# A two-FFN transformer block on one core: the low halves of the second FFN's gate and up products by seven products in place of eight

## The reference

```python
x = x + 0.5 * ffn(layernorm(x), w_gate_up, w_proj)
x = x + attention(layernorm(x), w_qkv, w_proj, b_proj)      # linear attention, 16 heads of 32
x = x + 0.5 * ffn(layernorm(x), w_gate_up, w_proj)

def ffn(x, w_gate_up, w_proj):
    wq = ternary_quant(w_gate_up)            # groups of 64: +-scale or 0, in bf16
    gate, up = split(x @ wq.T)               # 512 -> 2 x 2048
    h = silu(gate) * up
    hn = rms_norm(h)
    return hn @ ternary_quant(w_proj).T      # 2048 -> 512
```

## Time and profile before

| | us |
|---|---|
| median of 3 runs | 875.66 |
| lowest, highest run | 872.84, 879.67 |
| the profiled execution | 873.84 |
| its span, first to last instruction | 871.2 |
| PE busy | 852.2 |
| DVE busy | 511.7 |
| ACT busy | 443.0 |
| POOL busy | 71.5 |

### The profile page before, as it was taken

One profiled execution on the slowest core, in us unless ns is written; L12 is line 12 of the kernel. 1 busy time (PEld: TensorE's weight loads), 2 busy tenths in 40 slices (PEclk: granted clock), 3 DMA queues, 4 the chain that ended last, 5 costly groups with the idle time before them and its releaser, 6 DMA issues. The chain is left out here.

```text
span 871.2 us, 13142 instructions
## 1 busy us (share of the span) xinstructions
PE 852.2 (98%) x4932; PEld 413.3 (47%) x4998; DVE 511.7 (59%) x979; ACT 443.0 (51%) x822; POOL 71.5 (8%) x114
## 2 busy tenths in 40 slices
PE   6999999999999989999999999999999999999998
PEld 5544444444444434464646464444444444444445
DVE  7999997824347566657696958433443443432332
ACT  7976667536435555556657463543444344334331
POOL 2211001200010010000000000000000000000000
PEclk9999999999999999999999999999999999999999
DMA  9999508996747679960505062163433343333236
GB/s 262 179 182 125 76 1 169 216 223 185 163 117 149 112 147 196 185 125 1 86 1 86 1 147 97 21 113 73 73 73 72 73 73 73 73 73 61 61 69 136
DMA packets 257486, 94.70 MB, mean 109 GB/s; under 512 B 242832, under 2 KB 245648, under 8 KB 256400
## 3 DMA queue, kind: packets, MB, share of 16 engines
q1 hardware_dynamic: 248448, 73.42, 45.2%
q0 software_dynamic: 5024, 13.11, 6.7%
q10 hardware_dynamic: 3952, 7.34, 2.6%
HBM read 29.62 MB, written 8.39 MB: 44 GB/s over the span
## 5 line engine op out<-in xcount | busy, mean ns | idle before, releaser
L1643 PE MATMUL proj_ps<-down_w,slots 128*128 128x512 bf16 x910 | 202.9, 379 | 1.1 <-issue 0.2
L1172 DVE SCALAR_TENSOR_TENSOR slots<-up_ps,silu 128x512 f32<-128x512 f32 x117 | 80.9, 691 | 179.8 <-PE up_ps L1629 134.2
L1629 PE MATMUL gate_ps<-gu_w,xT 128*128 128x512 bf16 (+1 forms) x762 | 173.1, 368 | 3.1 <-ACT silu L809 2.3
L1629 PE MATMUL up_ps<-gu_w,xT 128*128 128x512 bf16 (+1 forms) x759 | 171.3, 366 | 0.9
L1643 PEld LDWEIGHTS proj_ps<-down_w,slots 128*128 128x128 f16 x928 | 90.7, 98 | 109.9 <-DVE xs L1194 0.8
L809 ACT ACTIVATE silu<-gate_ps 128x512 f32<-128x512 f32 x117 | 68.8, 588 | 142.9 <-PE gate_ps L1629 142.9
L819 ACT ACTIVATE o_buf<-slots 128x512 f32<-128x512 f32 x128 | 80.5, 629 | 113.7 <-DVE slots L1172 113.0
L1629 PEld LDWEIGHTS gate_ps<-gu_w,xT 128*128 128x128 f16 x776 | 74.0, 98 | 88.4 <-ACT silu L809 2.7
L1629 PEld LDWEIGHTS up_ps<-gu_w,xT 128*128 128x128 f16 x776 | 73.7, 98 | 84.4 <-issue 0.8
L1185 DVE SCALAR_TENSOR_TENSOR slots<-slots,inv 128x512 f16<-128x512 f32 x124 | 91.0, 744 | 3.7 <-ACT slots L830 3.6
L830 ACT ACTIVATE slots<-slots,inv 128x512 f16<-128x512 f32 x124 | 86.3, 711 | 11.1 <-POOL inv L709 7.6
(11 more groups left out here) (151 smaller groups left out, 942.4 us busy)
## 6 DMA issues: line engine op xcount, KB each, us to landing
gu_kept<-gu_w POOLq DMA_DIRECT2D x4, 1024.0 KB, 4.7
gu_w<-gu_kept POOLq DMA_DIRECT2D x4, 1024.0 KB, 6.2
out_dram<-xs SPq DMA_DIRECT2D x15, 256.0 KB, 2.4
xs<-in_L_attn_x_dram SPq DMA_DIRECT2D x3, 1024.0 KB, 8.5
aw<-in_L_attn_w_qkv_dram ACTq DMA_DIRECT2D x12, 256.0 KB, 2.9
slots<-in_L_ffn_w_gate_up_dram ACTq DMA_DIRECT2D x5, 512.0 KB, 6.7
aw<-in_L_ffn_w_gate_up_dram POOLq DMA_DIRECT2D x10, 256.0 KB, 5.5
aw<-in_L_ffn_w_proj_dram POOLq DMA_DIRECT2D x8, 256.0 KB, 5.5
```

The source lines that it names most:

```text
L1172: nc.vector.scalar_tensor_tensor(out=h_rows(i, q), in0=bank(up_ps, j), scalar=gu_out(i), in1=silu_rows(j), op0=ALU.mult, op1=ALU.mult).the ...
L1629: mm = nc.tensor.matmul(bank(ps, j)[:, first:first + width], xT(m)[:, t, r, k, :], gu_w[:, q, side, k, first:first + width], start=(k + r ...
L1643: mm = nc.tensor.matmul(proj_ps[:, use % 2, :], h_turned(i)[:, r, j, :], down_w[:, j, :], start=(r + j == 0), stop=(r == 1 and j == HC - 1))
```

## The change

The two low halves of x of two tiles, A = (a1 a2; b1 b2) with 256 rows of K each, times the gate and up weights (G1 U1; G2 U2) are a 2 x 2 product of blocks. The change makes it by seven products (Strassen's form in Winograd's order) in place of eight, for tiles 18 to 31 taken in pairs: 28 sets of one pair and one column block. A product is two matmuls of 512 columns; the high halves stay as they were, 16 matmuls a set. PE's step k makes the high products of set k (`x`, `y`, `v`, `w`, one PSUM bank each) between the low products of set k + 1.

The sums inside a set are made in PSUM: product 1 stands in bank y, ACT copies it to bank x (`seed_x`), products 6 and 5 are added in y with a copy kept after each (`hold_two` on DVE, `hold_four` on ACT), DVE writes the seed of bank w (`seed_w`) and adds to bank v (`join_v`).

It needs sums of the weights (four forms of 128x1024 per column block) and of x. The weight forms are made in tiles 8 to 10 of the first FFN (`weight_parts` on ACT, `weight_forms` on DVE), scaled by a power of two of the largest group mean (a second `partition_all_reduce` on POOL, behind `inverse(7)`), stored in DRAM (`keep_forms`, 4 x 1 MB) and brought back after attention (`bring_forms`). `low_halves(u)` makes the sums of x, five DVE operations for each pair. `row_sum`, `keep_weights` and all else of tiles 8 to 15 keep their places. `xT8` moves from `att_w` to a slot.

```diff
+SETS = 4 * (LAYER - 2) // 2
+FIRST_LOW = (1, 7, 6, 5, 2, 3, 4)
+IN_STEP = (1, 7, "x", 6, "y", 5, "v", 2, 3, "w", 4)
+LOW_BANK = {1: "y", 6: "y", 5: "y", 3: "y", 2: "x", 7: "v", 4: "v"}
...
@@ pool
+            pool.wait_ge(most_done, 1)
+            nc.gpsimd.partition_all_reduce(w_all, w_most, P, bass.bass_isa.ReduceOp.max).then_inc(all_done, 1)
             for i in range(EARLY, LAYER):
                 if i < 12:
                     rstd(3, i % TILES)
@@
                 inverse(i)
+                for n in {8: (0,), 9: (1, 2), 10: (3,)}.get(i, ()):
+                    keep_forms(n)
@@ scalar
+            def weight_parts(n):
+
+                q = FORMS_FIRST[n]
+                act.wait_ge(powers_done, 1)
+                if n:
+                    act.wait_ge(gform_done, 4 * n - 2)
+                for side in range(2):
+                    nc.scalar.activation(w_parts[side], gu_w[:, q, side, 0:2, :].rearrange("p k n -> p (k n)"),
+                                         ACT.Copy, scale=w_up).then_inc(parts_done, 1)
...
+            def step_of(k):
+                u, q = k // QH + 1, k % QH
+                if k + 1 < SETS:
+                    seed_x(k + 1)
+                if k:
+                    square_of(k - 1, 1)
+                silu_of(k, 0)
+                for n in highs_with(k)[:1]:
+                    h_high(*n)
+                if k + 1 < SETS:
+                    hold_four(k + 1)
+                silu_of(k, 1)
+                square_of(k, 0)
+                for n in highs_with(k)[1:]:
+                    h_high(*n)
+                if q == 1 and u < 6:
+                    for i in (LAYER + 4 + 2 * u, LAYER + 5 + 2 * u):
+                        x_high(*group_place(i))
@@ ffn_tile on scalar
+                    for n in {(8, 2): (0,), (9, 0): (1,), (9, 2): (2,), (10, 0): (3,)}.get((i, q), ()):
+                        weight_parts(n)
@@ vector
+            def weight_forms(n, second):
...
+                for k, (to, rows, by, other, op) in enumerate(made):
+                    if second:
+                        dve.wait_ge(gform_done, 4 * n + 2 + k)
+                    else:
+                        dve.wait_ge(parts_done, 2 * n + 1 + k)
+                    nc.vector.scalar_tensor_tensor(out=to, in0=rows, scalar=by, in1=other, op0=ALU.mult, op1=op)\
+                      .then_inc(gform_done, 1)
...
+            def hold_two(k):
+
+                dve.wait_ge(item_done, item_no(k, 6))
+                nc.vector.tensor_copy(held_two, set_bank(k, "y")).then_inc(two_held, 1)
+
+            def seed_w(k):
+
+                dve.wait_ge(item_done, item_no(k, 7))
+                dve.wait_ge(four_held, k + 1)
...
+                nc.vector.tensor_tensor(set_bank(k, "w"), set_bank(k, "v"), held_four, ALU.add).then_inc(w_seeded, 1)
+
+            def join_v(k):
+
+                dve.wait_ge(two_held, k + 1)
+                nc.vector.tensor_tensor(set_bank(k, "v"), set_bank(k, "v"), held_two, ALU.add).then_inc(v_joined, 1)
...
+            def step_of(k):
+                u, q = k // QH + 1, k % QH
+                new = [group_place(i) for i in (LAYER + 4 + 2 * u, LAYER + 5 + 2 * u)] if u < 6 else []
+                if k and projected_with(k - 1) is not None:
+                    ffn_out(projected_with(k - 1))
+                if q == 2:
+                    for n in new[:1]:
+                        x_low(*n)
+                if k + 1 < SETS:
+                    hold_two(k + 1)
+                inner(k, 0)
...
+                if k + 1 < SETS:
+                    seed_w(k + 1)
+                    join_v(k + 1)
+                for n in highs_with(k)[:1]:
+                    h_low(*n)
+                inner(k, 1)
...
+                if q == 3:
+                    mean_squares(LAYER + 2 * u)
+                    if new:
+                        low_halves(u + 2)
+                if q == (0 if u == 1 else 1):
+                    for n in new:
+                        ln_stats(*n)
+                if q == 1:
+                    for n in new:
+                        ln_apply(*n)
@@ ffn_tile on vector
+                    for n, second in {(8, 2): ((0, 0),), (8, 3): ((0, 1),), (9, 0): ((1, 0),), (9, 1): ((1, 1),),
+                                      (9, 2): ((2, 0),), (9, 3): ((2, 1),), (10, 0): ((3, 0),),
+                                      (10, 1): ((3, 1),)}.get((i, q), ()):
+                        weight_forms(n, second)
+                    if (i, q) == (LAYER, 0):
+                        low_halves(1)
@@ tensor
+            for k in range(SETS):
+                for it in IN_STEP:
+                    if isinstance(it, str):
+                        high_products(k, it)
+                    elif k + 1 < SETS:
+                        low_product(k + 1, it)
+                if projected_with(k) is not None:
+                    project(projected_with(k))
```

More of the change, by code:

```diff
@@ L770, in _ @@
             bring_weights(3)
-            for i in range(LAYER, FFN_TILES):
-                if i < LAYER + 3 * TILES:
-                    rstd((i - LAYER) // TILES + 9, i % TILES)
-                inverse(i)
+            for q in range(QH):
+                pool.wait_ge(forms_saved[q], 16)
+            pool.wait_ge(prod_done, product_no(BLOCKS - 1, 2, 4))
+            pool.wait_ge(summed_done, summed_no(BLOCKS - 1, "c21", 2))
+            for q in range(QH):
+                bring_forms(q)
+            for i in (LAYER, LAYER + 1):
+                rstd(9, i % TILES)
+                inverse(i)
+            for u in range(1, 8):
+                if u > 1:
+                    inverse(LAYER - 1 + 2 * u)
+                if u < 6:
+                    for i in (LAYER + 4 + 2 * u, LAYER + 5 + 2 * u):
+                        rstd(*group_place(i))
+                inverse(LAYER + 2 * u)
+            inverse(FFN_TILES - 1)
         @block.scalar
@@ new lines, in hold_four, with silu_of @@
+            def hold_four(k):
+                act.wait_ge(item_done, item_no(k, 5))
+                if k:
+                    act.wait_ge(w_seeded, k)
+                else:
+                    act.wait_ge(rden_done, HPG * BLOCKS)
+                nc.scalar.activation(held_four, set_bank(k, "y"), ACT.Copy).then_inc(four_held, 1)
+            def silu_of(k, side):
+                act.wait_ge(item_done, item_no(k, "xv"[side]))
+                if k:
+                    act.wait_ge(inner_done, 2 * k - 1 + side)
+                else:
+                    act.wait_ge(up_used, 4 * LAYER + 7 + side + CREDIT)
+                nc.scalar.activation(silu[:, side, :], set_bank(k, "xv"[side]), ACT.Silu, scale=GU_OUT)\
+                  .then_inc(silu_done, 1)
@@ L1116, in _ @@
                 output_high(BLOCKS - 1, h)
-            for i in range(LAYER, FFN_TILES):
-                ffn_tile(i, (i - LAYER) // TILES + 9 if i < LAYER + 3 * TILES else None)
-            for q in range(QH):
-                h_high(FFN_TILES - 1, q)
+            for i in (LAYER, LAYER + 1):
+                ffn_tile(i, 9)
+            for k in range(SETS):
+                step_of(k)
+            square_of(SETS - 1, 1)
+            for i in (FFN_TILES - 2, FFN_TILES - 1):
+                for q in range(QH):
+                    h_high(i, q)
         @block.vector
@@ L1598, in _ @@
             att_out(BLOCKS - 2, 3)
-            for i in range(LAYER, FFN_TILES):
-                ffn_tile(i, (i - LAYER) // TILES + 9 if i < LAYER + 3 * TILES else None)
-            for q in range(QH):
-                h_low(FFN_TILES - 1, q)
-            ffn_out(FFN_TILES - 2)
+            for i in (LAYER, LAYER + 1):
+                ffn_tile(i, 9)
+            for k in range(SETS):
+                step_of(k)
+            mean_squares(FFN_TILES - 1)
+            for i in (FFN_TILES - 2, FFN_TILES - 1):
+                for q in range(QH):
+                    h_low(i, q)
+            for i in range(FFN_TILES - 4, FFN_TILES - 1):
+                ffn_out(i)
             ffn_out_last()
@@ new lines, in high_products @@
+            def high_products(k, where):
+                (m, t), side = group_place(two_tiles(k)["vw".count(where)]), "yw".count(where)
+                if where == "w":
+                    pe.wait_ge(w_seeded, k + 1)
+                for c in range(DC):
+                    mm = nc.tensor.matmul(set_bank(k, where), xT(m)[:, t, 0, c, :], gu_w[:, k % QH, side, c, :], start=False,
+                                          stop=(c == DC - 1), skip_group_check=True)
+                mm.then_inc(item_done, 1)
```

280 lines of the change are left out of this document (254 added, 26 removed).

## The result

The changed kernel takes 878.76 us (median of 15 runs, 875.23 to 886.64) beside 873.68 us (15 runs, 871.97 to 879.67) for the kernel before on the same chip: a ratio of 1.0057 with a 95% interval from 1.0033 to 1.0082. It is slower by about 5 us, within the 1% that the forecast called no change. The forecast was 878.2 us.

The account below looks back on a forecast made before the run. PE was taken as the bound, busy 98% of 871.2 us, with ACT just ahead in tiles 8 to 10. Terms -12.1 + 9.1 + 1.8 + 1.9 + 1.8 = +2.5 us on a 875.66 median gave 878.2 us, range 868 to 888.

Parts of the forecast that it names:

- Removed, 12.1 us: Second FFN, low halves: 28 sets lose two matmuls each, 56 x 0.216 = 12.1 us, all of it counting.
- Tiles 8 to 10, 9.1 us: First FFN: added ACT and DVE work delays silus PE waits for, 9.1 us lost, bounds 6 and 13.
- The sequence on ACT: Tiles 8 to 10: ACT's queue carried on from 187.29 with 3.1 us loads, silu (10,1) ending at 231.4.
- rival 3: Tiles 9, 10 and steps: slower by clock falls (+1.7), late loads (+4), dearer PSUM writes (7), 891 us; chance 0.17.
- The all-reduce: POOL, behind inverse(7): the new all-reduce takes 13 us, ends at 179.1, starts silu (8,2) 0.6 us late.
- rival 2: Tiles 8 to 10: load 2 lands early, added work is hidden, gain arrives, 868.5 or 863.6 us; under 866.9: 0.14.
- Tile 16, 1.8 us: Attention, tile 16: low_halves(1) on DVE ahead of att_out delays PE by 1.8 us, bounds 1.2 and 2.3.
- hold_two, 1.9 us: New steps: the DVE copy of 0.69 us delays product 5 by 0.08 us in some 24 steps, 1.9 us.
- Three single stalls, 1.8 us: New steps: low_halves(2) before the first hold_two 0.6, layer-norm statistics 0.2, x_high holding seed_x 1.0, together 1.8 us.
- The clock swinging in the steps (4): New steps: short waits make the clock swing, 1.7 us in each of 27 steps, +46 us, 920; chance 0.04.

Follow-up runs that it names:

- e8: Changed kernel with weight forms made in tiles 10 and 11, first low_halves behind att_out, hold_two on ACT in place of DVE: 861.84 us, ratio 0.9856.
- e1: Changed kernel without weight_parts, weight_forms and keep_forms, the kept weights fetched as forms, output not the reference's: 866.07 us, ratio 0.9929.
- e4: Changed kernel with the first low_halves moved behind the four att_out of tile 16: 879.49 us, ratio 1.0084.

## Why the prediction was right, and where it was not

The number fits to 0.6 us, and part of that is luck: I put my sum of +2.5 us on a median of three runs, 875.66, where 15 runs give 873.68. By differences, +2.5 was forecast and +5.1 measured. By its steps:

- **Removed, 12.1 us: right.** In e8, where nearly every wait of the steps is gone, stretch B is 10.85 us shorter than before; 0.9 us are `seed_x` at the second step, still there in e8 (582.74 against 581.82 by the pace), and some 0.3 are not placed.
- **Tiles 8 to 10, 9.1 us: too small, 12.4 us; this is the mis-sized term.** The 9.1 is by how much PE starts (10,3) later than before, in absolute time. Measured, it starts at 232.30 in place of 222.56, 9.7 us later, and behind it the clock takes 2.7 more. (The 13.8 us of stretch A hold another 1.4, by which PE came to tile 9 sooner; a PE that is 1.4 us ahead waits 1.4 us more for the same silu, and the span neither gains nor loses by it.) The bounds of 6 and 13 hold it, and the first FFN ended 12 us late where I had 7 to 11.
  - *The sequence on ACT* ended near the forecast: the silus of (9,1), (10,0) and (10,1) were put at 204.8, 224.55 and 231.4 and end at 204.85, 224.73 and 232.24. That is in part luck. The silu of (9,0) was put at 199.85 and ended at 197.83, so PE's first wait was 0.9 us in place of 1.7; and the load beside `keep_forms(0)` took 4.96 us where I had 3.1. Two misses of about 2 us cancel in the silu of (9,1).
  - *The clock* is what failed: I had computed waits of 2.55 and 3.4 us, knew the row of 2.26 us with half clock behind it, and the sum held no clock; I had it as rival 3, at 1.7 us. A fall cost 2.7 us here. Behind the first it took the place of the 2.55 us wait for the next silu (that wait is not in the trace: one of the two is absorbed, as the rival had it); behind the second nothing absorbed it. The last silu 0.8 us later than put and the 2.7 us make the 3.3 us between 9.1 and 12.4, to 0.2.
- **The all-reduce:** POOL showed 5.60 us ahead and 7.05 behind, close to the 5.63 and 7.11 of the earlier trace rows. Its effect on PE in e1, where it stays, is 0.3 us, within the spread of A. Passing on 0.6 us of delay to the silu of (8,2) was wrong: load 2 took 5.7 us (178.94 to 184.62) where it had taken 7.2, and the silu started at 185.63, before at 187.29. So rival 2 had a point in its favour, but far from its 3.1 us.
- **Tile 16, 1.8 us: right in kind,** 1.6 us by e4.
- **hold_two, 1.9 us: right.** The copy takes 0.691 us, as the row of 0.690 had it. By the Trainium skill (VectorE: DVE Perf Modes, the errata table) it would be an estimated 0.66 us; the measurement decides for the row. e8, with a copy that is 0.09 us shorter, gave back 2.35 us over all 28 sets.
- **Three single stalls, 1.8 us: too much.** `seed_x` cost 0.9 in place of 1.0; product 5 of the first two steps (584.23, 590.82) was late by 0.17 and 0.1 where I had 0.6 and 0.2. The balance of B is -12.1 + 1.6 + 2.35 + 1.25 = -6.9, against my -12.1 + 1.8 + 1.9 + 1.8 = -6.6; the 1.25 is the remainder of the first point, not a measurement of its own. So of the 2.6 us between +2.5 and +5.1, tiles 8 to 10 are 3.3, B is -0.3, and -0.4 lie between tile 11 and the attention, not placed.
- **Rivals.** That the gain arrives (2) fell with the waits. That the clock decides (3) was half right: one fall of the clock went into the time, without the dear PSUM writes of that rival. These take 0.70 us on DVE and 0.58 on ACT, no more than reads. The clock swinging in the steps (4) did not occur: 1.00 in all windows from 550 us, with 0.08 us of waiting in nearly every step. The Trainium skill (TensorE: Matmul & The Clock Gate, the second failure mode) warns of that pattern; no run here shows it.

What stays open: why the clock falls after one wait of 3 us and not after another; the records show that it does, not what decides. And what makes the rest of the spread from 875 to 887 us: the mean clock goes with most of it, but the slowest run has the clock of the median one. That a load issued just ahead of a store is quick and one issued just behind it slow is a reading of four traces, tested by no run of its own.

## What to carry to other kernels

Work added to an engine beside the critical one costs by its place in that engine's queue, not by its amount: eight operations of 1.1 us on ACT, with those on DVE and the transfers that go with them, cost stretch A 12 to 14 us behind row sums that wait for their loads, 4.6 ahead of them, and nothing two tiles later. Count three things in such a place together: the work, the transfers that it sets off beside the loads it stands behind, and the clock behind a long wait (nine waits of 2.0 us or more stand in these traces; seven had a fall of the clock, at 1.7 to 2.7 us each). And where a wait of 0.08 us stands in every step, look at both chains before reordering: moving it only moved the loss, the shorter copy on the other engine removed it.
